# Two cross-attention layers over 32 sequences: transposed copies loaded, layer one's value bias as a matmul, ScalarE normalises

## What is computed

```python
# layer "0" (L0_xattn)                     # M = 256 context rows, E = 512
q = x @ Wq + bq ; k = ctx @ Wk + bk ; v = ctx @ Wv + bv
w = softmax((q @ k.T) / sqrt(E), axis=1)   # over the x rows
x = w @ v + x
x = (x - mean(x)) * rsqrt(var(x) + 1e-6) * gamma + beta
# layer "1" (L1_xattn)
Q = x @ Wq + bq ; K = ctx @ Wk + bk ; V = ctx @ Wv + bv
weights = softmax((Q @ K.T) / sqrt(512), axis=-1)
out = x + (weights @ V) @ Wo + bo
```

## Time and profile before

| | us |
|---|---|
| median of 3 runs | 721.43 (720.66 to 721.87) |
| profiled execution | 719.84 |
| its span, first to last instruction | 717.8 |
| TensorE busy | 687.4 (96%) |
| VectorE busy | 597.1 (83%) |
| GpSimd busy | 489.5 (68%) |
| ScalarE busy | 426.6 (59%) |

### The profile page before, as it was taken

One profiled execution on the slowest core, in us unless ns is written; L12 is line 12 of the kernel. 1 busy time (PEld: TensorE's weight loads), 2 busy tenths in 40 slices (PEclk: granted clock), 3 DMA queues, 4 the chain that ended last, 5 costly groups with the idle time before them and its releaser, 6 DMA issues.

```text
span 717.8 us, 12706 instructions
## 1 busy us (share of the span) xinstructions
PE 687.4 (96%) x4107; PEld 596.5 (83%) x4107; DVE 597.1 (83%) x1362; ACT 426.6 (59%) x1009; POOL 489.5 (68%) x391
## 2 busy tenths in 40 slices
PE   8997999999999999999999999999999999999987
PEld 6875978988797898879788887978888798888876
DVE  4898698897979789797978879797887979798865
ACT  2644747657484765748476574847557484756632
POOL 0177776948486795848678584858868485886753
PEclk9998999999999999999999999999999999999999
DMA  8802004040210404021040403004040300301003
GB/s 287 299 1 64 25 1 147 2 146 0 79 67 0 146 0 146 0 95 51 0 146 0 146 0 114 32 7 139 0 146 0 126 21 25 121 0 59 1 0 118
DMA packets 30336, 49.50 MB, mean 69 GB/s; under 512 B 2160, under 2 KB 10352, under 8 KB 30320
## 3 DMA queue, kind: packets, MB, share of 16 engines
q1 hardware_dynamic: 30320, 49.29, 20.5%
HBM read 32.51 MB, written 16.78 MB: 69 GB/s over the span
## 4 chain that ended last, share of the span: by engine, by line
PE 74%; DVE 19%; issue 3%; POOL 3%; DMA 1%; ACT 1%; SPq 0%; DVEq 0%; POOLq 0%
PE bank L385 61%; PE bank L392 12%; DVE n L1007 6%; DVE stats L996 3%; DVE pc_lo L803 2%; DVE var_eps L1003 2%; DVE x_odd L991 1%; DVE x_even L991 1%; PE bank L405 1%; POOL x_even L1198 1%; DMA wk_sb<-in_L_xattn_Wk_dram 1%; DVE rb L918 1%; DVE n L827 1%; POOL wq_sb L1158 1%; POOL wq_sb L1154 1%
## 5 line engine op out<-in xcount | busy, mean ns | idle before, releaser
L1185 POOL TENSOR_TENSOR prod<-n,u_b 128x512 f32<-128x512 f32 x64 | 81.6, 1296 | 5.9 <-ACT prod L716 5.9
L801 DVE SCALAR_TENSOR_TENSOR y_lo<-bank,terms,y_hi 128x512 fp32r<-128x512 f32 x64 | 45.6, 749 | 37.1 <-ACT y_hi L630 37.1
L1214 POOL TENSOR_TENSOR r<-r,beta_b 128x512 f32<-128x512 f32 x60 | 76.3, 1300 | 0.0
L1207 POOL TENSOR_TENSOR r<-n,gamma_b 128x512 f32<-128x512 f32 x60 | 75.6, 1288 | 0.0
L632 ACT ACTIVATE xT_hi<-bank 128x512 fp32r<-128x512 f32 x64 | 33.0, 605 | 70.5 <-PE bank L392 70.5
L630 ACT ACTIVATE y_hi<-bank,terms 128x512 fp32r<-128x512 f32 x64 | 42.0, 679 | 52.0 <-PE bank L385 51.9
L385 PE MATMUL bank<-wvo_hi,pc_hi 128*128 128x512 f32 x128 | 52.2, 408 | 15.8 <-DVE pc_lo L803 15.8
L1177 POOL TENSOR_TENSOR rstd<-var_eps,minus_half 128x2 f32<-128x2 f32 x32 | 22.3, 697 | 62.1 <-DVE var_eps L1003 60.5
L726 ACT ACTIVATE e<-e 128x512 f32<-128x512 f32 x60 | 37.8, 630 | 35.6 <-POOL e L1170 35.0
L1146 POOL TENSOR_TENSOR cn_even_lo<-ctxn,cn_even_hi 128x1024 fp32r<-128x1024 f32 x8 | 19.2, 2395 | 56.6 <-ACT cn_even_hi L740 56.6
L385 PE MATMUL bank<-xT_hi,wqk_hi 128*128 128x512 f32 x128 | 52.8, 412 | 1.1 <-DVE xT_lo L803 1.1
(11 more groups left out here) (198 smaller groups left out, 2475.6 us busy)
## 6 DMA issues: line engine op xcount, KB each, us to landing
out_dram<-r SPq DMA_DIRECT2D x15, 1024.0 KB, 5.0
x_even<-in_x_dram SPq DMA_DIRECT2D x8, 1024.0 KB, 7.5
ctxn<-in_ctx_dram SPq DMA_DIRECT2D x16, 512.0 KB, 4.0
x_odd<-in_x_dram SPq DMA_DIRECT2D x8, 1024.0 KB, 7.0
wq_sb<-in_L_xattn_Wq_dram SPq DMA_DIRECT2D x4, 256.0 KB, 3.7
wk_sb<-in_L_xattn_Wk_dram SPq DMA_DIRECT2D x2, 512.0 KB, 7.3
wv_sb<-in_L_xattn_Wv_dram SPq DMA_DIRECT2D x2, 512.0 KB, 9.4
wq_sb<-in_L_xattn_Wq_dram SPq DMA_DIRECT2D x1, 1024.0 KB, 11.3
```

The source lines that it names most:

```text
L801: i = dve.scalar_tensor_tensor(dst, src, bias, high.bitcast(F32), ALU.add, ALU.subtract)
L1185: pool.tensor_tensor(prod[j % 2][:], N[:, j, :], u_b[1][:], ALU.mult).then_inc(prod_ready, 1)
L1207: pool.tensor_tensor(r[:, j, :], N[:, j, :], gamma_b[:], ALU.mult).then_inc(scaled_ready, 1)
L1214: pool.tensor_tensor(r[:, j, :], r[:, j, :], beta_b[:], ALU.add).then_inc(resid_ready, 1)
```

## The change

Four things.

- **Transposed copies.** x and the context come a second time from HBM, already transposed (`x_turned`, `ctx_turned`), and so do the weights. TensorE's 24 transposes of a pair are gone. `x_raw` is a new buffer; the transposed context lands in the buffer of `e1`. ScalarE rounds x in two instructions of 128x1024 (`round_xT`) and the context in one (`round_cT`), from SBUF; VectorE cuts the low part of x in two instructions of 128x1024 (`cut_xT`), GpSimd that of the context in one (`cut_cT`). x is cut a pair ahead, in the middle of the iteration.
- **Layer one's bias as a matmul** (the value bias of the layer that runs first). The row sums stay a row: ScalarE rounds 96 partitions of the tile, VectorE writes the low part of 32 of them (`rs_rows`), and each `pr` tile gets a seventh product, `rs_rows` x `bv_rows`, of 96 rows and 512 columns. `add_w_lo`, L1113, `bias_of_rows` and `add_bias` are gone; `row_sums` has four products for three.
- **Bias terms of the weights** are products of one column on TensorE (`term_columns`) and no longer dot products on VectorE.
- **ScalarE normalises**: `normalise` moves from VectorE to ScalarE, with a shift of minus mean times rstd in front (two instructions of 128x1 per half); VectorE writes `minus_mean`.

The order of the engines is written by hand before and after. ScalarE's `row_terms` 2 and 3 now stand behind `y1_hi`, the two `xT_hi` and the tiles of `wc` and `rs`. PSUM tiles rotate over seven banks (`ROUND = 7`) for eight. SyncE issues four loads per pair for two.

```diff
+    bank = {t: turn % ROUND for turn, t in enumerate(STEADY)}
...
+            def term_columns(it, L, wqT, wkT, bq):
+                dst = begin(it, f"t{L}")
+                columns = ([(wqT[:, :, k * P:(k + 1) * P], bk_col[L]) for k in range(KD)]
+                           + [(wkT[:, :, c * P:(c + 1) * P], bq) for c in range(KC)]
+                           + [(bk_col[L].unsqueeze(2).to_broadcast([P, KD, P]), bq)])
+                for n, (w, v) in enumerate(columns):
+                    for e in range(KD):
+                        mm = pe.matmul(dst[:, n:n + 1], w[:, e, :], v[:, e:e + 1], start=e == 0, stop=e == KD - 1)
...
-                pe.wait_ge(w_lo_added, it.times(1, 1))
+                pe.wait_ge(w_lo, it.times(2 * RM, 2 * RM))
                 dst = begin(it, "rs")
-                end(product(dst[:], [(ones_r[:], W[0][:, :, mt, :]) for mt in range(RM)] + [(ones_r[:], w_lo_sum)]),
-                    "rs")
+                end(product(dst[:], [(ones_r[:], w[:, :, mt, :]) for w in W for mt in range(RM)]), "rs")
...
+                if name == "pr":
+                    if j == 0:
+                        wait_emptied(pe, it, "rs")
+                    terms.append((rs_rows[:BV_ROWS, j * P:(j + 1) * P], bv_rows[:BV_ROWS]))
...
+            def round_xT(it, h, ahead):
+                act.wait_ge(x_raw_loaded, it.times(16, 16 + 16 * ahead))
+                act.activation(XT[0][:, 2 * h:2 * h + 2, :], x_raw[:, 2 * h:2 * h + 2, :], ACT.Copy)\
+                   .then_inc(hi["xT"], 1)
...
+            def normalise(it, j):
+                if j % RT == 0:
+                    act.wait_ge(mean_ready, it.times(2, j // RT + 1))
+                    act.wait_ge(rstd_ready, it.times(2, j // RT + 1))
+                    for n in range(j, j + RT):
+                        act.activation(shift[:, n:n + 1], minus_mean[:, n:n + 1], ACT.Copy,
+                                       scale=rstd[:, n:n + 1]).then_inc(shift_ready, 1)
+                act.wait_ge(shift_ready, it.times(J, j + 1))
...
+                act.activation(N[:, j, :], XN[it.parity][:, j, :], ACT.Identity, bias=shift[:, j:j + 1],
+                               scale=rstd[:, j:j + 1]).then_inc(n_ready, 1)
...
+            def cut_xT(it, h, ahead):
+                dve.wait_ge(hi["xT"], it.times(2, 2 * ahead + h + 1))
+                dve.tensor_tensor(XT[1][:, 2 * h:2 * h + 2, :], x_raw[:, 2 * h:2 * h + 2, :],
+                                  XT[0][:, 2 * h:2 * h + 2, :].bitcast(F32), ALU.subtract).then_inc(xT_lo, 1)
```

More of the change, by code:

```diff
@@ L463, in prepare1c @@
                         dst = begin(it, "bo1")
-                        end(product(dst[:], [(ones_r[:].bitcast(F32), wq1_sb[:, 0, :])]), "bo1")
-            def transpose_inputs(it):
-                xn = XN[it.parity]
-                pe.wait_ge(x_loaded[it.parity], it.loads())
-                for k in range(KD):
-                    transposes(it, "xT", k, [xn[:, j, k * P:(k + 1) * P] for j in range(J)])
-                pe.wait_ge(ctx_loaded, it.times(16, 16))
-                for c in range(KC):
-                    transposes(it, "cT", c, [ctxn[:, j, c * P:(c + 1) * P] for j in range(J)])
+                        end(product(dst[:], [(ones_r[:].bitcast(F32), bv_wo_sb[:, 0, :])]), "bo1")
             def transpose_n(it):
@@ L501, in scores0 @@
                     wait_emptied(pe, it, "y", c)
-                for c in range(KC):
-                    wait_emptied(pe, it, "cT", c)
+                pe.wait_ge(cT_lo, it.times(1, 1))
                 for b in range(2):
@@ L859, in prepare0 @@
+            def prepare0(it):
+                for h in range(2):
+                    cut_xT(it, h, 0)
                 low_wqk(it, 0, lambda k: SCALE)
+                wait_filled(dve, it, "t0")
+                dve.tensor_scalar(terms[0][:], at(("t0", 0))[:, :KD + KC + 1], SCALE, None, ALU.mult)\
+                   .then_inc(emptied[BANK["t0", 0]], 1)
             def prepare1a(it):
-                dve.wait_ge(loaded["cols"], 16 * 2)
-                dve.tensor_scalar(gscale[:], gamma_col[:], SCALE, None, ALU.mult).then_inc(gscale_ready, 1)
+                dve.wait_ge(loaded["cols"], 16)
+                dve.tensor_scalar(gscale[:], gamma_col, SCALE, None, ALU.mult).then_inc(gscale_ready, 1)
@@ L1037, in norm_and_output @@
                 if it.front:
-                    if it.back:
-                        wait_filled(dve, it, "nT", KD - 1)
-                        dve.wait_ge(scaled_ready, it.times(J, 0))
-                    normalise(0)
-                    normalise(1)
                     add(3)
@@ L1068, in norm_and_output @@
                     output(it, 2)
-                if it.front and not it.before_last:
-                    normalise(2)
-                    normalise(3)
                 if it.back and not it.before_last:
@@ L1079, in iteration @@
                 begin_it = it.j is None and it.known == 0
+                more = it.j is not None or it.known < PAIRS - 1
                 if begin_it:
@@ L1082, in iteration @@
                 if it.front:
-                    for k in range(KD):
-                        low(it, "xT", k, XT[1][:, k, :], XT[0][:, k, :], per=KD)
-                    for c in range(KC):
-                        low(it, "cT", c, CT[it.parity][1][:, c, :], CT[it.parity][0][:, c, :], per=KC)
                     row_terms0(it)
@@ L1225, in iteration @@
                         scale_n(it)
[L1226 to L1229 removed]
+                    add_beta(it, range(J))
                 if it.j is None and it.known == 0:
                     bv_wo()
[L1232 to L1235 removed]
                 more = it.j is not None or it.known < PAIRS - 1
```

400 lines of the change are left out of this document (180 added, 220 removed).

## The result

| | before | after |
|---|---|---|
| median, us | 721.04 of 4 runs (719.75 to 721.87) | 882.15 of 4 runs (880.56 to 884.42) |
| ratio | | 1.224, 95% interval 1.2205 to 1.2272 |
| span of the profiled execution | 717.8 | 882.6 |
| up to the first `n` transposes | 73.95 | 95.13 |
| the loop, 14 pairs | 582.50 (41.61 a pair) | 715.55 (51.11 a pair) |

The direction was forecast, the size was not: +161 us for +25. Between the two profiled executions it is +165, of which +133 are in the loop, +21 in the start and +10.6 in the last full pair.

The account below looks back on a forecast made before the run. TensorE's list plus its waits bounds a pair: 41.61 - 1.46 (list) - 1.4 (`pc_lo`) + 1.6 + 2.8 (port tolls) = 43.15 us. 14 pairs +21.6, start +2.3, end +0.5: 746 us, range 702 to 766.

Parts of the forecast that it names:

- A rule read from rows in which the waiting engine always won: Shared SBUF port: VectorE and GpSimd alternate, one instruction each, 0.94 us a turn; tolls 1.6 (`w_lo`) and 2.8 us (`pt`) a pair.

Follow-up runs that it names:

- e7: Changed kernel, but GpSimd waits for `w_lo` before `scale_n`, ScalarE writes `r1s` and `neg1`, `xT` cut behind first statistics, `bv_wo` waits for first `r0s`: 723.19 us, ratio 1.0044.

## What to carry to other kernels

A wait that an engine makes for another may be the only moment at which a third gets in: before moving or deleting one, list all that the shared resource still has to let through in that stretch, tiny instructions on a critical chain first. Where GpSimd and VectorE both work on SBUF, don't give GpSimd ten ready instructions in a row; a semaphore between any two (0.12 to 0.17 us each) bounded VectorE's wait by one instruction, and in e7 a pause put where VectorE's chain runs, with small instructions moved to ScalarE, was better still. A rule read from rows in which the waiting engine always won says nothing about the cost of losing; a range needs a price for that too.
